# TensorE's semaphore increments in front of its product groups, taken out of a four-block graph network kernel

## The chip, the cores and the metric

One core of one Trainium2 chip runs the whole program in one launch. The metric is the device time of that launch in microseconds (us).

## The reference

The graph has 6,250 nodes with 16 features and 206,250 edges (100,000 in both directions, and a loop on each node), sorted by destination. Four blocks follow one another, each as `x = layernorm(x + block(x))`:

```python
# L0: messages from a tensor product of node and edge features, summed by destination row
m = silu(einsum('ei,ej,ijh->eh', x[src], edge_attr_8, W_msg_tp) * n1) @ W_msg_lin * n2
agg = segment_sum(m, row, n_nodes)
# ... update by a second tensor product of x and agg, silu, linear, residual

# L1: six graph convolutions (16-64-128-64, linear layers 64-32-3-32-64, then 64-128-64-16), leaky, tanh
agg = segment_sum(h[src] * norm[:, None], dst) + h * (dinv * dinv)[:, None]

# L2: maxima
h = segment_max(x[src] * edge_weight1, dst);  h @ W.T + b

# L3: two rounds; a 16x16 matrix for every edge out of a 13-32-256 network, mean, GRU
w = relu(edge_attr_13 @ w1 + b1) @ w2 + b2
m = einsum('ei,eio->eo', hx[src], w.reshape(-1, 16, 16))
hx = gru_cell(segment_sum(m, dst) * inv_deg[:, None], hx)
```

## The kernel before

The program is written engine by engine, each engine with its own list of instructions, and the engines meet only at semaphores. The edges stand in tiles of 128, and a batch is HT = 8 tiles; there are NB = 202 batches. Everything over the edges goes batch by batch, with buffers in pairs (`h = k % 2`), and gathers and sums are made as products with matrices of zeros and ones.

**The messages stage** (320 to 3,253 us in the profile) runs `messages` (lines 1003 to 1035) in a loop on the chip of 50 rounds of SL = 4 batches, and two batches behind it. For batch k TensorE does, in this order: `expand` for batch k+1 (L977, the tensor product on gathered rows); `compare` (L985) with `early` true; then three times (i = 0, 1, 2) 16 products of 392 columns that add placed messages into two banks (L1030), and ahead of the third of them `compare` with `early` false. ScalarE counts equal codes out of each `compare` in `count_equals` (L1310, four tiles each time), and VectorE turns the counts into places (L1933), casts, multiplies (L1888, L1905) and sums. GpSimd scatters finished rows (L859). Each `compare` waits until ScalarE has read the banks that it writes; each of the three parts of L1030 waits for a step of VectorE (HOTS, PLACE1, PLACED).

**The graph convolutions** (3,335 to 5,000 us) stream an adjacency matrix through a ring of buffers: `sum_block` (L1100) multiplies blocks of 28 tiles, its first product waiting for the block's transfer; `combine` (L1111) follows every group of blocks.

**Pass 7** (5,150 to 6,890 us, maxima) and **passes 8 and 9** (7,034 to 9,050 and 9,155 to 11,200 us, the two rounds of L3) gather rows with `gather8` (L900), turn them with `turn8` (L909), and add segments with `segments` (L885), whose output columns come from registers. `maxima` and `messages8` call these. In `messages8` TensorE makes the 16x16 matrices (L1234 for the bias, L1238) in two groups of banks as VectorE (L2287) has used the matrices of the batch before; VectorE multiplies and reduces (L2287, L2295), ScalarE compares indices (L1493, L1499), GpSimd gathers node rows (L841).

**The semaphore of this case.** `pe_go` (L349) is incremented by TensorE itself, by `pe.sem_inc(pe_go, 1)`, behind the waits that stand ahead of a group of products. It stands on 12 lines: 882 (`segments`), 896 (`gather8`), 1011, 1015, 1019 and 1026 (`messages`), 1068 (once), 1091 (`sum_block`), 1109 (`combine`), 1192 and 1201 (`maxima`) and 1232 (`messages8`). No engine waits for `pe_go`. `turn8` has waits without it, and so have `sum_block`'s waits for a transfer. VectorE has a semaphore of the same kind, `dve_go`.

The rows below name engines: PE is TensorE's products, PEld its weight loads, PEldq the records of TensorE's sequencer (the part of an engine that takes the program's instructions in order and hands them on) such as a separate semaphore instruction, SPq SyncE's issues of transfers.

Of the kernel before, what the change touches and what calls it, by code (L numbers as in the profile page):

```python
# [107 lines left out]
def build(nc, a, out):  # L108
# [12 lines left out]
    with ctx:  # L121
# [3 lines left out]
        def sem(name):  # L125
# [41 lines left out]
               for x in (arena[:, 6 * HE:6 * HE + HE // 2], acc[:, 4 * P:4 * P + HE // 2])]  # L167
# [112 lines left out]
                for j in range(2)]  # L280
# [65 lines left out]
        left_open = sem("left_open")  # L346
        hot8_made, picked, selected, turned, copied = [{p: sem(f"{x}{p}") for p in range(7, NPASS)}
                                                       for x in ("hot8_made", "picked", "selected", "turned", "copied")]
        pe_go = sem("pe_go")  # L349
        dve_go = sem("dve_go")  # L350
        r_out = sem("r_out")
        numbered = sem("numbered")
# [517 lines left out]
        def _(pe):  # L870
# [5 lines left out]
            def segments(p, k, h):  # L876

                pe.load(out_at, base[0:1, ds(k * HT + HT, HT)])
                outs = [pe.snap(r, min_val=0, max_val=2 * CH - 32) for r in out_at]
                pe.wait_ge(scl[p].sem, scl[p].at(k - 1, APER[p]))  # L880
                pe.wait_ge(vec[p].sem, vec[p].at(k + 1, LOWS7 if p == 7 else LOWS8))
                pe.sem_inc(pe_go, 1)
                for u in range(HT):
                    for x in (masked[h], rests[h], lows[h]):
                        last = mm(sums[:, ds(outs[u], 32)], hot[h][:, u, :], upper(x)[:, u * 32:(u + 1) * 32],  # L885
                                  start=False, stop=False)
                last.then_inc(ten[p].sem, 1)

            def gather8(p, j):

                if p == 7:
                    pe.wait_ge(hot8_made[p], j + 1)
                else:
                    pe.wait_ge(hot8_in[j % 2], hot8_count(p, j))
                pe.wait_ge(selected[p], j)
                pe.sem_inc(pe_go, 1)
                rows, hots = picked_rows[:, 0:gathers(p, j) * P], hot_of(p, j)
                for b in range(LAST):
                    for i in range(3):
                        mm(rows, x8[:, b, i, :], hots[:, b, :], start=b == i == 0, stop=False)  # L900
                last = mm(rows, x8[0:STACKED, LAST, 0, :], hots[0:STACKED, LAST, :], start=False, stop=True)
                last.then_inc(picked[p], 1)
# [99 lines left out]
            def messages(it, b, last_batch):  # L1002
                k, h = it * SL + b, b % 2
                pe.wait_ge(vec[0].sem, vec[0].at(k, HOTT))
                pe.wait_ge(vec[0].sem, vec[0].at(k, PROD))
                if last_batch:
                    pe.wait_ge(ten[0].sem, ten[0].at(k - 1, TPER[0]))
                    pe.sem_inc(ten[0].sem, 2)
                else:
                    pe.wait_ge(nodes_in[1 - h], nth(it, b + 1, 16 * HT))  # L1010
                    pe.sem_inc(pe_go, 1)
                    expand(k + 1, 1 - h)
                    pe.wait_ge(codes_in[1 - h], nth(it, b + 1, 16 * HT // R))
                    pe.wait_ge(scl[0].sem, scl[0].at(k, LATE_EQ + HT - 1))
                    pe.sem_inc(pe_go, 1)
                    compare(k + 1, 1 - h, True)
                for i, step in enumerate((HOTS, PLACE1, PLACED)):
                    pe.wait_ge(vec[0].sem, vec[0].at(k, step))
                    pe.sem_inc(pe_go, 1)
                    if i == 2:  # L1020
                        if last_batch:
                            pe.wait_ge(ten[0].sem, ten[0].at(k, LATE - 1))
                            pe.sem_inc(ten[0].sem, 1)
                        else:
                            pe.wait_ge(scl[0].sem, scl[0].at(k, EARLY_EQ + R - 1))
                            pe.sem_inc(pe_go, 1)
                            compare(k + 1, 1 - h, False)
                    for u in range(HT):
                        for half in range(2):
                            last = mm(halves[half], placed[h][:, i, u, :, :].rearrange("p a f -> p (a f)"),  # L1030
                                      hot_b[h * HT + u][:, half * (NB8 // 2):(half + 1) * (NB8 // 2)],
                                      start=False, stop=False)
                last.then_inc(ten[0].sem, 1)
# [31 lines left out]

            pe.wait_ge(agg_in, 1)
            pe.wait_ge(lin_open, 1)
            pe.sem_inc(pe_go, 1)
            spread_group(0)
            spread_group(1)  # L1070
            pe.wait_ge(positions, 4)
# [13 lines left out]
            def sum_block(p, G, j):  # L1085

                rows, W, par = piece(p), 3 * FEATURES[p], G % 2
                g, n = group_number(p, G), block_number(p, G, j)
                if p > 1 and G == 0:
                    chunks_done(pe, PHASES[p], min((j * SC + SC - 1) // 4, NC - 1), WAVES[PHASES[p]])  # L1090
                    pe.sem_inc(pe_go, 1)
                if j == 0:
                    if g >= 2:
                        pe.wait_ge(sum_vec, group_step(g - 2, REDUCED))
                    for bank in range(2):
                        mm(ps[:, 2 * par + bank, 0:2 * W], zero16[:, 0:P], zero16[:, 0:2 * W], start=True, stop=False)
                pe.wait_ge(blocks[n % RING], 16 * (n // RING + 1))
                for s in range(SC):
                    for u in range(GB):
                        last = mm(ps[:, 2 * par + u // 2, u % 2 * W:(u % 2 + 1) * W], ring[n % RING][:, s, u * P:(u + 1) * P],  # L1100
                                  rows[:, j * SC + s, :, :].rearrange("p k f -> p (k f)"),
                                  start=False, stop=(j == NCH - 1 and s == SC - 1 and u % 2 == 1))
                last.then_inc(blocks_used, 1)

            def combine(p, G):

                F, par = FEATURES[p], G % 2
                pe.wait_ge(sum_vec, group_step(group_number(p, G), REDUCED))
                pe.sem_inc(pe_go, 1)
                for u in range(GB):  # L1110
                    last = mm(ps[0:F, 6, u * P:(u + 1) * P], part[par][:, u * F:(u + 1) * F], pick[par][:, u, :],  # L1111
                              start=True, stop=True)
                last.then_inc(combined, 1)
# [67 lines left out]
            def maxima(k):  # L1181
# [7 lines left out]
                    turn8(p, k + AHEAD)  # L1189
                pe.wait_ge(loaded[h], load_count(p, k))  # L1190
                pe.wait_ge(scl[p].sem, scl[p].at(k - 1, RELU7))
                pe.sem_inc(pe_go, 1)
                for i in range(STRIPS):
                    last = mm(ps[32 * i:32 * i + 32, 7, 0:SE], w["f1"][32 * i:32 * i + 13, :], edges[h][32 * i:32 * i + 13, :],
                              start=True, stop=True)
# [2 lines left out]
                    gather8(p, k + AHEAD + 1)  # L1198
                segments(p, k - 1, 1 - h)
                pe.wait_ge(vec[p].sem, vec[p].at(k, SCAN))  # L1200
                pe.sem_inc(pe_go, 1)
                nc.tensor.transpose(ps[:, 6, 0:P], wk[:, HE:HE + P], w["ident"][:, :]).then_inc(ten[p].sem, 1)

            for k in range(NB):
# [14 lines left out]
            for p in (8, 9):  # L1219
# [6 lines left out]
                def messages8(k):  # L1226
# [2 lines left out]
                    pe.wait_ge(loaded[h], load_count(p, k))  # L1229
                    for strips, used in ((range(2), MUL[1]), (range(2, STRIPS), MUL[3])):  # L1230
                        pe.wait_ge(vec[p].sem, vec[p].at(k - 1, used))
                        pe.sem_inc(pe_go, 1)
                        for i in strips:
                            mm(ps[:, 4 + i, :], ones16[32 * i:32 * i + 32, :],  # L1234
                               bias3[32 * i:32 * i + 32, :].unsqueeze(1).to_broadcast([32, 2, 256]), start=True, stop=False)
# [1152 lines left out]
```

## Time and profile before

| | |
|---|---|
| time before, median of 3 runs | 11252.9 us |
| the three runs | 11252.9, 11231.1, 11258.11 us |
| the profiled execution | 11253.09 us |
| its span | 11251.3 us |
| granted TensorE clock over the span | 0.855 of full speed |
| TensorE products / weight loads busy | 79% / 51% of the span |
| VectorE / GpSimd / ScalarE busy | 55% / 40% / 32% |

The span is the stretch from the first to the last instruction; 1.8 us of the profiled execution's own time lie around it. Busy time is the time in which an engine executes; the time of a separate semaphore instruction isn't in it. No engine is busy throughout, so what sets the time is read from waits: what an engine waited for, and which part of a hand-off from one engine to the next is work.

### The profile page before, as it was taken

How to read it: one execution, taken by the hardware profiler on the slowest of the kernel's cores; microseconds unless marked ns; L12 is line 12 of the kernel's file. 1: busy time of each engine (PE TensorE's matmuls, PEld its weight loads, DVE VectorE, ACT ScalarE, POOL GpSimd, SP SyncE). 2: the span in 40 equal slices, each digit the busy share in tenths (PEclk: the TensorE clock that was granted, in tenths of full speed). 3: DMA queues.
4: the chain of work that ended last, by engine and by line, in shares of the span. 5: the costliest groups of instructions: out<-in, count | busy, mean ns of one | idle time of the engine just before them, and what ended most of it. 6: DMA issues, size and time to landing. Idle time of an engine off the chain costs nothing. (4 is left out here: it accounts for less than half of the span.)

```text
span 11251.3 us, 211389 instructions
## 1 busy us (share of the span) xinstructions
PE 8897.2 (79%) x72779; PEld 5698.2 (51%) x72910; DVE 6144.4 (55%) x11833; ACT 3561.2 (32%) x10701; POOL 4484.3 (40%) x4575
## 2 busy tenths in 40 slices
PE   0588888888878999956888885888788858788887
PEld 0345544555556878843444443555444535455544
DVE  2577766777753232223555553665666636666666
ACT  4234322333320010002444443333333323333334
POOL 1455555556530000005444553444444334444442
PEclk9899988899986999957888887888888878888888
DMA  9422233222239878973555553333333423333333
GB/s 317 151 76 81 80 86 88 80 80 80 80 122 368 311 251 313 337 310 116 157 158 159 159 159 108 109 105 106 107 105 108 113 68 105 108 105 107 106 107 90
DMA packets 998418, 1625.38 MB, mean 144 GB/s; under 512 B 253394, under 2 KB 787598, under 8 KB 997174
## 3 DMA queue, kind: packets, MB, share of 16 engines
q1 hardware_dynamic: 808244, 1542.53, 41.8%
q0 software_dynamic: 146240, 27.89, 3.0%
q10 hardware_dynamic: 43202, 44.90, 1.2%
q8 instruction: 496, 8.13, 0.3%
q14 instruction: 236, 1.93, 0.1%
HBM read 1324.07 MB, written 289.76 MB: 143 GB/s over the span
## 5 line engine op out<-in xcount | busy, mean ns | idle before, releaser
L841 POOL DMA_INDIRECT arena<-tab,x_all x2902 | 2747.6, 947 | 5074.9 <-DMA tab<-stage 2026.1
L859 POOL DMA_INDIRECT adj<-acc x1616 | 1683.0, 1041 | 1288.5 <-DVE acc L1933 747.2
L900 PE MATMUL ps<-invdeg,acc 128*128 128x384 bf16 (+1 forms) x5377 | 1369.2, 413 | 224.1 <-issue 216.2
L900 PE MATMUL ps<-dinv,acc 128*128 128x384 bf16 (+1 forms) x5404 | 1267.9, 387 | 324.5 <-issue 259.0
L1310 ACT ACTIVATE wide<-ps,not_all 128x128 bf16<-128x128 f32 x1616 | 658.2, 419 | 1535.6 <-remote 993.0
L900 PEld LDWEIGHTS ps<-invdeg,acc 128*128 128x128 bf16 x5454 | 621.3, 120 | 939.7 <-issue 738.7
L900 PEld LDWEIGHTS ps<-dinv,acc 128*128 128x128 bf16 x5454 | 591.0, 114 | 962.1 <-issue 745.6
L1493 ACT ACTIVATE arena<-w_iota,rel 128x128 f32<-128x128 f32 x3232 | 987.9, 388 | 13.5
L2287 DVE TENSOR_TENSOR dinv<-ps,arena 128x512 f32<-128x512 f32 x808 | 519.1, 684 | 784.6 <-remote 778.8
L2287 DVE TENSOR_TENSOR arena<-ps,arena 128x512 f32<-128x512 f32 x808 | 519.2, 684 | 725.8 <-remote 708.6
L1499 ACT ACTIVATE acc<-arena,unit 128x1024 bf16<-128x1024 f32 x303 | 347.9, 1148 | 1744.4 <-PE ps L1238 894.6
L1499 ACT ACTIVATE arena<-arena,unit 128x1024 bf16<-128x1024 f32 x303 | 347.9, 1148 | 1659.0 <-PE ps L1238 689.7
L977 PE MATMUL ps<-arena 128*128 128x128 f32 x3232 | 481.8, 289 | 381.1 <-issue 198.1
L909 PEld LDWEIGHTS ps<-x_all,dinv 128*128 128x128 f32 x3892 | 578.6, 222 | 397.6 <-issue 242.1
L909 PE MATMUL ps<-x_all,dinv 128*128 128x16 f32 x3892 | 640.3, 291 | 168.6 <-issue 121.9
L1888 DVE TENSOR_TENSOR arena<-ps,threes 128x1024 bf16<-128x1024 f32 x606 | 718.7, 1212 | 0.0
L1238 PE MATMUL ps<-w_w2b,arena 32*128 32x256 f32 x6464 | 668.4, 463 | 2.6 <-issue 2.4
L1100 PE MATMUL ps<-x_all,arena 128*128 128x192 bf16 (+1 forms) x8232 | 591.5, 233 | 91.9 <-DMA arena<-adj 91.7
L977 PEld LDWEIGHTS ps<-arena 128*128 128x128 f32 x3232 | 432.3, 200 | 446.3 <-issue 322.8
L1100 PE MATMUL ps<-arena 128*128 128x192 bf16 (+1 forms) x8232 | 602.1, 237 | 48.4 <-DMA arena<-adj 48.3
L1100 PEld LDWEIGHTS ps<-x_all,arena 128*128 128x128 bf16 x8232 | 553.3, 102 | 155.6 <-DMA arena<-adj 103.2
L1724 DVE SCALAR_TENSOR_TENSOR dinv<-x_all,ps 128x384 f32<-128x384 f16 (+1 forms) x606 | 384.0, 634 | 454.0 <-issue 218.3
(357 smaller groups left out, 14006.6 us busy)
## 6 DMA issues: line engine op xcount, KB each, us to landing
arena<-adj SPq DMA_DIRECT2D x588, 896.0 KB, 5.6
arena<-rels SPq DMA_DIRECT2D x202, 512.0 KB
arena<-tab SPq DMA_DIRECT2D x1616, 64.0 KB
invdeg<-hot_rows_of SPq DMA_DIRECT2D x150, 672.0 KB
dinv<-hot_rows_of SPq DMA_DIRECT2D x100, 896.0 KB
adj<-zero SPq DMA_DIRECT2D x28, 3136.0 KB
dinv<-hot_rows_of SPq DMA_DIRECT2D x102, 672.0 KB
x_all<-src_parts SPq DMA_DIRECT2D x202, 256.0 KB
```

The source lines that it names most:

```text
L841: pool.indirect_dma_start(G[b][:, u, :], None, TABLE[PHASES[p]], bass.IndirectOffsetOnAxis(ap=idx[:, t:t + 1], axis=0)).then_inc(gathered[ ...
L859: pool.indirect_dma_start(adj_cells, bass.IndirectOffsetOnAxis(ap=pair[:, t, 0:1], axis=0), pair16[:, t, 2:3], None).then_inc(celled[g], 16)
L900: mm(rows, x8[:, b, i, :], hots[:, b, :], start=b == i == 0, stop=False)
L909: last = mm(turned_rows[:, u * 16:(u + 1) * 16], picked_by[j % 2][:, u * P:(u + 1) * P], pick_f, start=True, stop=True)
L977: last = mm(ps[:, 2 + u // 4, (u % 4) * P:(u % 4 + 1) * P], hotT[h][:, u * P:(u + 1) * P], nodes0[h][:, u, :], start=True, stop=True)
L1100: last = mm(ps[:, 2 * par + u // 2, u % 2 * W:(u % 2 + 1) * W], ring[n % RING][:, s, u * P:(u + 1) * P], rows[:, j * SC + s, :, :].rearran ...
L1238: last = mm(ps[:, 4 + i, v * 256:(v + 1) * 256], strip[h][32 * i:32 * i + 32, v * P:(v + 1) * P], w["w2b"][32 * i:32 * i + 32, :], start=F ...
L1310: act_fn(junk[u % 2][:, 0:(u % R + 1) * P], equal_to(u), ACT.Relu, bias=not_all[:, :], accum_out=equals[h][:, u:u + 1]).then_inc(scl[0].se ...
L1493: last = act_fn(far2[:, u, :], w["iota"][:, :], ACT.Square, scale=-1.0, bias=r[:, tile(k, u):tile(k, u) + 1])
L1499: act_fn(hot[h][:, :, :], far2[:, :, :], ACT.Relu, scale=-2.0, bias=unit[:, :]).then_inc(scl[p].sem, 1)
L1888: tt(placed[h][:, i, :, :, :], hot_a[:, :, :].unsqueeze(3).to_broadcast([P, HT, A8, 16]), threes[h][:, :, i, :].unsqueeze(2).to_broadcast( ...
L2287: tt(products[h][:, q * 512:(q + 1) * 512].rearrange("p (u o i) -> p u o i", u=2, i=16), ps[:, 4 + q, :].rearrange("p (u o i) -> p u o i", ...
```

## The change

All twelve `pe.sem_inc(pe_go, 1)` and the semaphore itself are taken out. No product, no wait, no transfer and no line of another engine is changed, and the order of TensorE's products and weight loads is the same.

```diff
@@ segments
                 pe.wait_ge(scl[p].sem, scl[p].at(k - 1, APER[p]))
                 pe.wait_ge(vec[p].sem, vec[p].at(k + 1, LOWS7 if p == 7 else LOWS8))
-                pe.sem_inc(pe_go, 1)
                 for u in range(HT):
@@ gather8
                 pe.wait_ge(selected[p], j)
-                pe.sem_inc(pe_go, 1)
@@ messages
                     pe.wait_ge(nodes_in[1 - h], nth(it, b + 1, 16 * HT))
-                    pe.sem_inc(pe_go, 1)
                     expand(k + 1, 1 - h)
                     pe.wait_ge(codes_in[1 - h], nth(it, b + 1, 16 * HT // R))
                     pe.wait_ge(scl[0].sem, scl[0].at(k, LATE_EQ + HT - 1))
-                    pe.sem_inc(pe_go, 1)
                     compare(k + 1, 1 - h, True)
                 for i, step in enumerate((HOTS, PLACE1, PLACED)):
                     pe.wait_ge(vec[0].sem, vec[0].at(k, step))
-                    pe.sem_inc(pe_go, 1)
...
                             pe.wait_ge(scl[0].sem, scl[0].at(k, EARLY_EQ + R - 1))
-                            pe.sem_inc(pe_go, 1)
                             compare(k + 1, 1 - h, False)
@@ sum_block
                     chunks_done(pe, PHASES[p], min((j * SC + SC - 1) // 4, NC - 1), WAVES[PHASES[p]])
-                    pe.sem_inc(pe_go, 1)
@@ combine
                 pe.wait_ge(sum_vec, group_step(group_number(p, G), REDUCED))
-                pe.sem_inc(pe_go, 1)
@@ maxima
                 pe.wait_ge(scl[p].sem, scl[p].at(k - 1, RELU7))
-                pe.sem_inc(pe_go, 1)
...
                 pe.wait_ge(vec[p].sem, vec[p].at(k, SCAN))
-                pe.sem_inc(pe_go, 1)
                 nc.tensor.transpose(ps[:, 6, 0:P], wk[:, HE:HE + P], w["ident"][:, :]).then_inc(ten[p].sem, 1)
@@ messages8
                         pe.wait_ge(vec[p].sem, vec[p].at(k - 1, used))
-                        pe.sem_inc(pe_go, 1)
                         for i in strips:
```

What the lines become is seen in the two built programs. An instruction there holds one wait. Before, the waits ahead of an increment go, with the increment, into a separate semaphore instruction. Without the increment the wait stands on the next instruction, which is the first weight load of the group; where a group waits for two semaphores, one separate semaphore instruction stays, with one of the two waits, and the other wait stands on the weight load (in `segments`, on the first of the register instructions that work out the output columns). So the separate instruction is gone at L1015, L1019 and L1026 in all batches, at L1011 in about three of four, at L1109, at L1201, at five of the 35 of L1091, and in the second of the two groups of a batch of L1232. It stays, without its increment, at `segments`, at `gather8`, at L1192 and in the first group of L1232.

## Rows read from the trace of the kernel before

**Rows 1.** The page, busy time, share of the span and number of instructions.

```profile
PE 8897.2 (79%) x72779; PEld 5698.2 (51%) x72910; DVE 6144.4 (55%) x11833; ACT 3561.2 (32%) x10701; POOL 4484.3 (40%) x4575
```

**Rows 2.** Windows by stage: length, engines' busy us (instructions), clock, DMA share, GB/s.

```profile
320.00:3253.00 2933.00, 2427.53 (x14437) 1450.68 (x14438) 2031.42 (x3649) 941.47 (x3936) 1667.18 (x1600) 0.90 0.30 84
3335.00:5000.00 1665.00, 1460.06 (x17808) 1255.79 (x17809) 449.94 (x1053) 122.67 (x247) 0.00 (x0) 0.87 0.89 324
5150.00:6890.00 1740.00, 1514.34 (x11942) 822.76 (x12016) 961.31 (x3201) 802.13 (x2222) 818.19 (x860) 0.85 0.53 159
7034.00:9050.00 2016.00, 1640.29 (x13873) 1018.57 (x13898) 1255.23 (x1816) 749.35 (x2018) 854.50 (x906) 0.84 0.38 106
9155.00:11200.00 2045.00, 1642.34 (x13870) 1027.14 (x13895) 1251.04 (x1811) 747.80 (x2018) 872.56 (x926) 0.83 0.37 105
```

**Rows 3.** By source line, `messages`: semaphore instructions, ns min/median/max, first and last start.

```profile
L1011 PEldq EVENT_SEMAPHORE  x201: 51/51/51, 325.9 to 3249.3; - x101
...
L1015 PEldq EVENT_SEMAPHORE  x201: 51/51/2512, 329.9 to 3252.0; - x101
...
L1019 PEldq EVENT_SEMAPHORE  x606: 51/51/51, 330.4 to 3269.3; - x152
...
L1026 PEldq EVENT_SEMAPHORE  x201: 51/51/51, 333.2 to 3257.3; - x101
```

**Rows 4.** By source line, convolutions and passes 7 to 9: the same columns.

```profile
L882 PEldq EVENT_SEMAPHORE  x609: 51/2397/4675, 5156.6 to 11204.1; - x153
...
L896 PEldq EVENT_SEMAPHORE  x606: 51/51/45266, 5057.5 to 11171.1; - x152
...
L1109 PEldq EVENT_SEMAPHORE  x84: 51/51/51, 3352.9 to 4998.5; - x84
...
L1201 PEldq EVENT_SEMAPHORE  x202: 51/51/51, 5161.5 to 6883.3; - x101
...
L1232 PEldq EVENT_SEMAPHORE  x808: 51/51/51, 7030.3 to 11196.3; - x162
```

**Rows 5.** Waits: engine, tile, line, what it waited for, us, times, longest.

```profile
ACT wide L1310 <- remote: 993.0, 147, 16.4
...
DVE dinv L2287 <- remote: 778.8, 186, 4.5
...
DVE arena L2287 <- remote: 708.6, 183, 4.3
...
PE ps L985 <- ACT wide L1310: 155.3, 170, 1.6
```

**Rows 6.** Timeline around 1273 us: start, duration, engine, line, and idle before.

```profile
1272.87 0.21 ACT L1310 ACTIVATION_READ_ACCUMULATOR wide<-ps,not_all 128x1 f32 x1
1273.19 0.14 PEld L985 LDWEIGHTS ps<-arena 22*128 22x128 bf16 x4 [1.09 <-issue]
```

**Rows 7.** Timeline around 8027 us, `turn8`, where no `pe_go` stands.

```profile
8026.32 0.60 DVE L1724 SCALAR_TENSOR_TENSOR dinv<-x_all,ps 128x384 f32<-128x384 f16 x1
...
8026.98 0.74 PEld L909 LDWEIGHTS ps<-x_all,dinv 128*128 128x128 f32 x6 [0.40 <-DVE dinv L1724]
```

**Rows 8.** Timelines of TensorE alone at 4200 and at 3600 us.

```profile
4199.82 4.78 PE L1100 MATMUL ps<-x_all,arena 128*128 128x192 bf16 x56
...
3599.76 10.48 PE L1100 MATMUL ps<-x_all,arena 128*128 128x192 bf16 x125
```

**Rows 9.** Timelines, 1247 to 1257 us and around 1272 us.

```profile
1247.30 8.22 SPq L750 DMA_DIRECT2D arena<-tab  x8
...
1250.44 0.34 PE L985 MATMUL ps<-arena 22*128 22x128 bf16 x4
...
1257.13 0.37 ACT L1310 ACTIVATE wide<-ps,not_all 128x128 bf16<-128x128 f32 x1 [6.62 <-remote]
...
1272.03 1.82 SPq L755 DMA_DIRECT2D arena<-bits  x4
```

**Rows 10.** Groups of weight loads: count, busy us, mean ns, idle before them.

```profile
L1030 PEld LDWEIGHTS ps<-acc,arena 128*128 128x128 bf16 x2424 | 265.3, 110 | 242.4 <-issue 115.4
```

More of the change, by code:

```diff
@@ L348, in build @@
                                                        for x in ("hot8_made", "picked", "selected", "turned", "copied")]
-        pe_go = sem("pe_go")
         dve_go = sem("dve_go")
@@ L1231, in messages8 @@
                         pe.wait_ge(vec[p].sem, vec[p].at(k - 1, used))
-                        pe.sem_inc(pe_go, 1)
                         for i in strips:
```

## The prediction

> **What bounds the kernel now.** The page's first part comes first: TensorE's products are busy for 79% of the span, its weight loads for 51%, VectorE for 55% [rows 1]. No engine fills the span, so the windows by stage come next [rows 2]. Each stage has TensorE busy for 81 to 88% of its length (2427.53 of 2933 us in the messages stage, 1642.34 of 2045 us in pass 9), in every case more than any other engine. But TensorE isn't simply the bound. The waits show that the other engines stand still for what TensorE makes, and TensorE for them: ScalarE's counting (L1310) waits 993.0 us in 147 long waits, VectorE's products with the edge matrices (L2287) 778.8 and 708.6 us, all of them "remote", which is a release that the trace has no record of [rows 5]. One of these in full: TensorE's comparison (L985) starts at 1250.44 and ends at 1250.78, and ScalarE's L1310, which needs nothing but that comparison and its own work before, starts at 1257.13, after 6.62 us of waiting [rows 9]. So some hand-offs arrive long after the product that makes them, and the chain product, hand-off, ScalarE or VectorE, hand-off back is what sets a batch. In the convolutions the transfers (DMA share 0.89, 324 GB/s [rows 2]) stand beside TensorE.
>
> Within that, the lines of this change are read from the separate semaphore instructions. One that lasts 51 ns found its wait met when it came to it; a longer one held TensorE's sequencer until its release. In the messages stage all 201 of L1011, all 606 of L1019 and all 201 of L1026 last 51 ns, L1015 up to 2512 ns [rows 3]. In the passes L882 is late as a rule (median 2397 ns, up to 4675), L896 seldom (median 51), L1201 and L1232 never [rows 4].
>
> **The change, part by part.** Counted in the built programs, about 1,853 separate instructions go: about 150 at L1011, 201 at L1015, 606 at L1019, 201 at L1026, 404 of the 808 at L1232, 202 at L1201, 84 at L1109, 5 at L1091. The others of these lines stay and only lose their increment.
>
> *The hand-off where the wait is late and the instruction goes (L1015).* ScalarE's last L1310 ends at 1272.87 + 0.21 = 1273.08, and the weight load that it releases starts at 1273.19: 0.11 us through a separate instruction [rows 6]. The nearest row with the wait on the weight load itself is `turn8`: VectorE ends at 8026.32 + 0.60 = 8026.92, and the load starts at 8026.98: 0.06 us [rows 7]. That is 0.05 us, or the length of the instruction itself (51 ns). TensorE waits for this release 170 times [rows 5], and there are 201 such instructions: between 170 x 0.05 = 9 us and 201 x 0.06 = 12 us. This hand-off lies on the chain of the batch: ScalarE's late counting ends, the early comparison runs, and ScalarE's next counting waits for it (L1310). I take 11 us.
>
> *The instructions whose wait is met long before (L1011, L1019, L1026, L1201, L1232, L1109).* They sit in the sequencer, ahead of the products that still run. A met wait costs the sequencer 51 ns, and the sequencer has at least 16 products of some 0.17 us each between two of them (four L1030 products take 0.84 us of record and the whole stage gives TensorE 14,437 products in 2933 us, 0.20 us each [rows 2]). The work that hides them is TensorE's own queue of products. If that cover isn't there, each costs its 51 ns: 1,853 x 0.051 = 95 us is the most that this can give back, and zero the least. The nearest row is that all of them stand at 51 ns in stretches where the products run on, so I take zero.
>
> *The instructions that stay (L882, L896, L1192, the first group of L1232).* L882 is the one late wait of passes 7 to 9, and it keeps its separate instruction, since it waits for two semaphores. What goes is an increment that nobody waits for. In the same instruction it adds no time that the rows show: nothing.
>
> *Waits on weight loads, new.* Could a weight load that carries a wait be worse than a plain one? The convolutions have such loads already: each block of 28 products begins with one, without `pe_go`. A run of 56 products, two blocks, takes 4.78 us, 85 ns each, and a run of 125, more than four blocks, takes 10.48 us, 84 ns each [rows 8]. If each met wait cost a load's 0.1 us, the second run would be some 0.4 us longer than 125 times the product's time within a block. I see nothing of that size, and take zero. Its bound is a whole exposed load, and stands under rival C.
>
> The sum: 11253.09 (the profiled execution, which is the median of 11252.9 within 0.2 us) - 11 = 11242 us. That is -0.1%, below the 0.3% that a measurement of this kernel can tell from no change (the three runs before already spread by 0.24%).
>
> **The rivals.**
>
> *A, the forecast: only L1015's hand-off shortens.* 11242 us; with the runs' own spread 11220 to 11260.
>
> *B, faster: late hand-offs shrink because TensorE's sequencer and the semaphores have less to do.* The 6.62 us of [rows 9] aren't explained by work. In that same stretch SyncE's issues of transfers come slowly too: eight in 8.22 us, where four take 1.82 us at 1272 [rows 9], 1.03 against 0.46 us each. Something that the engines share delays small instructions and hand-offs there, and many removed events may lighten it. A price in proportion: the messages stage has 14437 + 14438 + 3649 + 3936 + 1600 = 38,060 records of work [rows 2]; 1,158 instructions and 1,209 increments go, 6.2% of that number. 6.2% of the 993.0 us of late counting is 62 us. In passes 8 and 9 the records are 32,511 and 32,520, and 1,616 increments and 404 instructions go, 3.1%; of 778.8 + 708.6 = 1487.4 us that is 46 us. All of both with L1015's 11 gives -119, 11134 us. I center it with half of the passes' part, since VectorE's wait there has other work of the batch beside it: 11 + 62 + 23 = 96, 11157 us. For it: the lateness is the largest thing in the waits, and its cause is in no row. Against it: the share removed is small, and a shared delay needn't go in proportion.
>
> The Trainium skill has a rule that would give B its mechanism: the page "NOTIFIC — the notification-queue block", section 7.1, says that the internal path for the records of instructions always holds back its producers rather than lose a record, and that this can throttle an engine. By it each removed instruction is a record less. That the profiled execution's time equals the median doesn't settle it, since no run here shows whether the other runs carry the same records.
>
> *C, slower: a weight load that carries a wait isn't taken ahead of the products that run.* A plain load is hidden beside the product before it. If the one with the wait is held until the products before it are done, its length is exposed once for every group whose wait moved onto it: in the messages stage L1011, L1026 and three of L1019, 5 per batch. 5 x 202 x 0.110 us [rows 10] = 111 us, less L1015's 11: 11353 us. It decides at about 0.01 us per load: above that, L1015's gain is eaten. For it: before, the sequencer had passed the wait by the time the load was queued, so the load was free to go ahead; afterwards it may not be. Against it: the runs of [rows 8]. The stage is busy with products for 83% of its time, so an exposed load would mostly count. The page "TensorE: Matmul & The Clock Gate" of the Trainium skill, section "Step-by-step: what each phase is for", has TensorE's queue pull weight loads ahead of products in flight, on conditions of row groups and of the background buffer; it says nothing on loads that wait, so it leaves C open rather than supporting it.
>
> *D: the change does nothing that is seen*, because L1015's 0.05 us is lost in another wait of the batch: 11253 us. It is inside A's range.
>
> **How the numbers follow.** A 0.43, B 0.36, C 0.18, D 0.03. B's chance is that high because it needs only one part of a large unexplained quantity. The predicted time is A's, 11242 us. The range goes from 11134, B's far end, taken as 11130, to 11300, which holds A, D, nearly all of B, and the part of C in which half a load or less is exposed: 0.43 + 0.03 + 0.31 + 0.05 = 0.82. A's own range is 11220 to 11260. Faster by over 0.3% means below 11219: B, and a little of A, 0.37. Within 0.3%: A and D, with some of B's near end, 0.42. Slower by over 0.3%, above 11287: C with what is left, 0.21.
>
> **What would show it.** In the profile of the changed kernel, right for A: L985's load begins 0.06 us behind ScalarE's last L1310, where it was 0.11; the semaphore instructions of L1015, L1019 and L1026 are gone; the messages stage is shorter by about 10 us, and the other stages by less than 10 each. Right for B: the wait "ACT wide L1310 <- remote" well below 993 us, L2287's below 1487, and passes 8 and 9 shorter although their late wait, L882, stands as before. Right for C: a gap of 0.1 us or more ahead of the first L1030 product of a part, and the messages stage longer by 100 us. What would make the prediction wrong is that the late hand-offs react to TensorE's semaphore instructions at all, in either direction: their 2,480 us are more than two hundred times the term that I count.

## The result and the profile after

| | before | changed |
|---|---|---|
| time, median of 7 runs each | 11252.9 us | 11311.5 us |
| lowest and highest | 11231.1, 11284.0 | 11288.5, 11338.0 |
| ratio of changed to before | | 1.0048, 95% interval 1.0031 to 1.0064 |
| span of the profiled execution | 11251.3 us | 11302.2 us |

The changed kernel is slower by 0.5%, some 55 us. The forecast was 11242 us with a range of 11130 to 11300: the time lies outside, on the other side. All lines behind L882 have moved up: L985 is now L982, L1030 is L1023, L1310 is L1297, L2287 is L2274.

The page's first part shows no work added; TensorE's products are even busy for a little less [rows 1]:

```profile
PE 8868.1 (78%) x72779; PEld 5648.2 (50%) x72910; DVE 6138.1 (54%) x11833; ACT 3567.3 (32%) x10701; POOL 4480.1 (40%) x4575
```

Where the time went is told by stage, each from the first to the last start of one line in the profiled execution (L1030 for the messages, L1100, L1194, L2287):

| us | messages | convolutions | pass 7 | pass 8 | pass 9 |
|---|---|---|---|---|---|
| before | 2944.2 | 1662.3 | 1726.8 | 2010.3 | 2003.8 |
| changed | 3000.3 | 1668.0 | 1724.1 | 2000.9 | 2000.5 |

The messages stage lost 56 us, passes 8 and 9 gained 13 together. In the trace by source line, the fields behind the count are ns min/median/max of one and the first and last start; the first two rows are L1030 of before, the last two L1023 of the changed kernel:

```profile
L1030 PE MATMUL ps<-acc,arena x2424: 326/329/534, 341.7 to 3274.1; 128*128 128x392 bf16 x187
...
L1030 PE MATMUL ps<-arena x1212: 326/329/534, 330.5 to 3261.0; 128*128 128x392 bf16 x174
```

```profile
L1023 PE MATMUL ps<-acc,arena x2424: 326/329/535, 342.2 to 3330.7; 128*128 128x392 bf16 x187
...
L1023 PE MATMUL ps<-arena x1212: 326/329/534, 331.0 to 3319.2; 128*128 128x392 bf16 x174
```

The products themselves are as long as before; only the last starts 57 us later. The median batch isn't longer either: 14.15 us from one batch's first L1030 to the next before, 14.12 now, and 16 products of a part take 2.50 us from the first start to the last in both. What changed is the mean, 14.61 to 14.89: batches longer than 17 us were 12 of 201 and are 25. Seen by part, the 606 parts of 16 products exceed their 2.5 us by 235 us in sum before and by 343 us now, and the time between the parts is 52 us less: more of the lost time falls into the parts. The waits of the changed kernel (columns as in [rows 5]) put it down to late counting, as there:

```profile
ACT wide L1297 <- remote: 1095.0, 153, 16.7
...
DVE dinv L2274 <- remote: 780.0, 186, 4.6
DVE arena L2274 <- remote: 701.7, 182, 4.3
...
PEld ps L982 <- ACT wide L1297: 159.1, 139, 2.0
...
PE ps L982 <- ACT wide L1297: 123.4, 127, 1.6
```

ScalarE's wait on "remote" is 102 us longer than in [rows 5], VectorE's two are 5.7 us shorter in sum, and the products' own wait for ScalarE's last counting is 123.4 where it was 155.3. That last difference isn't the term of the forecast: 127 waits are put down to it instead of 170, and the mean of one rose from 0.91 to 0.97 us. The term is the hand-off itself, and it came as forecast. In the timeline of the changed kernel:

```profile
1288.46 0.21 ACT L1297 ACTIVATION_READ_ACCUMULATOR wide<-ps,not_all 128x1 f32 x1
1288.73 0.11 PEld L982 LDWEIGHTS ps<-arena 22*128 22x128 bf16 x4 [1.49 <-ACT wide L1297]
```

1288.46 + 0.21 = 1288.67, and the load starts 0.06 us later, where it was 0.11 [rows 6]. Over all groups that were released within 0.4 us, the median is 114 ns before (184 groups) and 51 ns now (160).

One of the new long batches looks like this (timeline of the changed kernel; start, duration, engine, line, idle before):

```profile
754.17 0.70 SPq L749 DMA_DIRECT2D arena<-tab  x1
...
754.92 0.33 PE L1023 MATMUL ps<-invdeg,arena 128*128 128x392 bf16 x1 [0.24 <-issue]
...
755.66 0.10 PEld L1023 LDWEIGHTS ps<-invdeg,arena 128*128 128x128 bf16 x1 [0.95 <-issue]
...
756.38 0.33 PE L1023 MATMUL ps<-invdeg,arena 128*128 128x392 bf16 x1 [1.13 <-issue]
...
757.09 0.10 PEld L1023 LDWEIGHTS ps<-invdeg,arena 128*128 128x128 bf16 x1 [1.33 <-issue]
...
757.81 0.33 PE L1023 MATMUL ps<-invdeg,arena 128*128 128x392 bf16 x1 [1.10 <-issue]
...
770.13 0.37 ACT L1297 ACTIVATE wide<-ps,not_all 128x128 bf16<-128x128 f32 x1 [16.51 <-remote]
```

Load, product, load, product come 0.7 us apart (755.66, 756.38, 757.09, 757.81) with no wait between them, for 16 us, and ScalarE gets TensorE's comparison only when it ends. The profile calls it "issue": TensorE waits for nothing that it shows. I call these **slow stretches**. [rows 9] shows the same in SyncE. Counted in the trace, gaps of 0.6 us or more between the starts of two products in the messages stage are 519 before and 609 in the changed kernel; in the convolutions, where GpSimd does nothing, gaps of 0.6 to 0.8 us are 6 in both.

### The profile page after: what moved, and what is told of

Same layout as the page of the kernel before. It is cut to its first block and busy times, and to the rows that moved or that the text cites. A ratio compares the mean times of both kernels' runs of the same rounds, so it can differ in the third digit from the quotient of the medians.

```text
span 11302.2 us, 209539 instructions
## 1 busy us (share of the span) xinstructions
PE 8868.1 (78%) x72779; PEld 5648.2 (50%) x72910; DVE 6138.1 (54%) x11833; ACT 3567.3 (32%) x10701; POOL 4480.1 (40%) x4575
## 5 line engine op out<-in xcount | busy, mean ns | idle before, releaser
L897 PE MATMUL ps<-invdeg,acc 128*128 128x384 bf16 (+1 forms) x5377 | 1333.2, 402 | 264.8 <-issue 165.3
L1297 ACT ACTIVATE wide<-ps,not_all 128x128 bf16<-128x128 f32 x1616 | 656.5, 418 | 1593.5 <-remote 1095.0
L2274 DVE TENSOR_TENSOR dinv<-ps,arena 128x512 f32<-128x512 f32 x808 | 518.4, 683 | 784.9 <-remote 780.0
L2274 DVE TENSOR_TENSOR arena<-ps,arena 128x512 f32<-128x512 f32 x808 | 518.5, 683 | 717.0 <-remote 701.7
L1091 PE MATMUL ps<-x_all,arena 128*128 128x192 bf16 (+1 forms) x8232 | 594.1, 234 | 93.6 <-DMA arena<-adj 93.5
L1225 PE MATMUL ps<-w_w2b,arena 32*128 32x256 f32 x6464 | 639.5, 449 | 0.7 <-issue 0.7
L1091 PE MATMUL ps<-arena 128*128 128x192 bf16 (+1 forms) x8232 | 603.1, 237 | 46.5 <-DMA arena<-adj 46.3
L1091 PEld LDWEIGHTS ps<-x_all,arena 128*128 128x128 bf16 x8232 | 556.0, 103 | 156.7 <-DMA arena<-adj 103.0
```

What stands on the lines that cost most here:

```text
L1225: last = mm(ps[:, 4 + i, v * 256:(v + 1) * 256], strip[h][32 * i:32 * i + 32, v * P:(v + 1) * P], w["w2b"][32 * i:32 * i + 32, :], start=F ...
L1297: act_fn(junk[u % 2][:, 0:(u % R + 1) * P], equal_to(u), ACT.Relu, bias=not_all[:, :], accum_out=equals[h][:, u:u + 1]).then_inc(scl[0].se ...
L2274: tt(products[h][:, q * 512:(q + 1) * 512].rearrange("p (u o i) -> p u o i", u=2, i=16), ps[:, 4 + q, :].rearrange("p (u o i) -> p u o i", ...
```

## The experiments

The runs came in sets, each on one chip with the kernel before beside them, and only within a set are times compared; in three sets there were hardly any slow stretches and the kernel before took 8,242 to 8,245 us, in the others it took 11,246 and 11,096 us.

### Which part: e1 to e4, a set without slow stretches

e1 takes out the increments of `messages` alone, e2 those of all other lines, e4 L1019 alone. e3 is the changed kernel with, at the four lines of `messages`:

```diff
-                    pe.sem_inc(pe_go, 1)
+                    pe.nop(nofuse=True)
```

which builds to the same separate semaphore instructions with their waits, without the increment.

> Only the four increments of `messages` (L1011, L1015, L1019, L1026) are taken out; the other eight stay. Theory W (a wait that moves onto a weight load in the messages stage, instead of standing in a separate instruction, brings more of the slow stretches): the whole of the change's +56 us in the messages stage, 11,305 to 11,320 us. Theory E (the change's loss is everywhere and the stages only differ by chance): half of it or less, 11,270 to 11,290 us. Theory I (the missing increments do it, not the place of the wait): as W.

> The eight increments outside `messages` are taken out, the four in it stay. Theory W: 11,240 to 11,255 us, the messages stage as before and passes 8 and 9 together up to 13 us shorter, as in the changed kernel. Theory E: 11,270 us or more.

> The changed kernel, but in `messages` each increment is replaced by an empty instruction that holds the wait: in the built program a separate semaphore instruction with the wait and without an increment, at the same 1,209 places. Theory W: the messages stage as in the kernel before, 11,240 to 11,255 us. Theory I (increments): the messages stage as in the changed kernel, 11,300 to 11,320 us.

> Only L1019 (the three waits of VectorE's steps ahead of the parts of L1030) loses its increment: 606 of the 1,158 separate instructions of the messages stage go. Theory W, each place alike: about half, +25 to +35 us, 11,280 to 11,290 us. Theory L (only the late wait L1015 matters, where TensorE's sequencer now runs on past the wait): no change, 11,245 to 11,260 us. Theory P (the loop's length and place in the code decide): any size, unrelated to the number of instructions.

Before 8245.3 us. Measured: e1 8244.6 (ratio 1.0000, 0.9991 to 1.0009), e2 8246.6 (0.9995, 0.9985 to 1.0004), e3 8243.5 (0.9998, 0.9988 to 1.0007), e4 8240.6 (0.9994, 0.9985 to 1.0003). None moves the time, so the set tells nothing of the 55 us, but much of what the 11,253 us are. The messages stage took 2,200 us instead of 2,944, pass 7 1,180 instead of 1,727, passes 8 and 9 about 1,265 each instead of 2,007; only the convolutions kept theirs (1,664 to 1,670 beside 1,662). In the messages stage of e1 gaps of 0.6 us or more are 8. And L1015, which I had read as late, is never late here. In e2 it is L1013:

```profile
L1013 PEldq EVENT_SEMAPHORE  x201: 51/51/51, 330.4 to 2512.0; - x101
```

### The change itself, and added records: f1 to f3, g1 to g4, sets without slow stretches

f1 and g4 are the changed kernel. f2 and f3 are the kernel before and the changed one, both with

```diff
+                        for _ in range(60):
+                            sp.sem_inc(extra, 1)
...
+                            if (i, u, half) != (2, HT - 1, 1):
+                                last.then_inc(extra, 1)
```

the first behind SyncE's loads of a batch, the second at L1030. g2 has `pe.nop(nofuse=True)` at all twelve lines, g1 eight further increments behind each L1019, g3 40 increments by ScalarE and those of the products.

> The changed kernel itself, beside the kernel before. In the runs of e1 to e4 the kernel before took 8,245 us, the late hand-offs of up to 16 us were all but absent, and no part of the change moved the time. Theory S (the +56 us of the changed kernel lies only in those slow stretches, where TensorE and SyncE take 0.7 us for each instruction): where they are absent, the changed kernel is within 0.2% of the kernel before, 8,235 to 8,255 us; where they are there, it is 0.3 to 0.6% slower in the messages stage alone. Theory T (all twelve together cost what no part alone costs): +40 to +60 us even without them.

> The changed kernel once more, beside the others of this set, since the kernel before has taken 11,253 us in one set of runs and 8,245 us in others. Where the set takes 8,245 us, no difference (within 0.2%). Where it takes 11,253 us, +40 to +70 us by every theory that takes the first measurement as it is; a theory that puts the +56 us down to chance expects less than 20 us.

f1: 8246.2 us, ratio 1.0002 (0.9993 to 1.0011); g4: 8250.8, 1.0007 (0.9997 to 1.0016). The messages stage is 2197.5 and 2197.1 us. Without slow stretches the change costs nothing that can be told, as theory S had it. The window of f1 over its messages stage (columns as in [rows 2]) shows why no hand-off counts there: TensorE is busy for 97% of it.

```profile
333.00:2530.00 2197.00, 2127.30 (x14497) 1351.47 (x14496) 1994.58 (x3653) 938.27 (x3941) 1627.45 (x1601) 0.98 0.42 112
```

> The kernel before, with semaphore increments that nobody waits for added in the messages stage: 60 by SyncE for each batch, behind its issues of transfers, and one by each of 47 of the 48 products of L1030. Theory R (the slow stretches come when the recording of instructions and semaphore changes has more than it can take; the trace of the kernel before kept 99,274 semaphore changes, that of e1 183,584): slow stretches of 0.7 us per TensorE instruction appear in the messages stage, which grows from 2,200 us by hundreds of us. Theory Q (the slow stretches have another cause): the messages stage stays within 30 us of 2,200 us.

> The changed kernel with the same added increments. Theory R, with the change's +56 us as something that slow stretches bring: longer than f2 by 20 to 100 us in the messages stage. Theory R, with fewer instructions to record as a gain: shorter than f2 by 20 to 100 us. Theory Q: equal to f2 within 15 us.

f2: 8764.1 us, f3: 8754.9 (4 runs each, ranges overlap). The messages stage grew to 2,710 and 2,708 us, but with 13 and 11 gaps of 0.6 to 0.8 us, where the trace of the kernel before in the first set has 191. What it waits for is another thing: SyncE's 60 instructions stand ahead of its next loads, and VectorE waits for those (L1905 of f2 is L1900 of the kernel before, the comparison that needs `rels`).

```profile
DVE arena L1905 <- DMA arena<-rels: 518.3, 141, 31.9
```

So f2 isn't the test that it was to be. What it shows is by accident: with late counting on the path without slow stretches, hand-offs at L985 of 113 ns (181 groups) in f2 and of 50 ns (178) in f3, the moved waits cost nothing either; f3 is shorter by 9 us, which is within the runs' spread. Nor does the hand-off's own saving show there: 180 times 63 ns would be 11 us, and the stages of the two traces differ by 2.

> All twelve increments replaced by an empty instruction that holds the wait: in the built program the same separate semaphore instructions as before, without their increments (as many as in the kernel before). With slow stretches in the runs: theory W (a wait on a weight load) expects the time of the kernel before, theory I (the increments) that of the changed kernel. Without them: no difference by either.

> The kernel before with eight more increments behind each L1019: 24 separate semaphore instructions more per batch, 4,824 in all, where the change takes away 1,158. If a separate instruction whose wait is met is hidden by the products queued ahead of it, as the prediction has it: no change, within 15 us. If each costs its 51 ns: +246 us. With slow stretches in the runs, and theory B (time in proportion to the instructions that TensorE's sequencer handles): +200 us or more.

> The kernel before with 40 increments more per batch by ScalarE between its late and its early counting, and one by nearly every product of L977 and L1030: some 95 semaphore changes and 40 instructions more per batch to record, and nothing at SyncE. Theory R (slow stretches come when recording can't keep up): slow stretches of 0.7 us per TensorE instruction, and the messages stage longer by more than 100 us. Theory Q (they have another cause): no such stretches; at most what ScalarE's 2 us per batch cost by themselves, 0 to 100 us.

g2: 8254.8 us, 1.0014 (1.0005 to 1.0024); g1: 8257.6, 1.0015 (1.0005 to 1.0024); g3: 8245.1, 0.9997 (0.9988 to 1.0007). g1's messages stage is 2,208 us, 11 us more than g4's, for 5,982 separate instructions more (4,824 added and the 1,158 that g4 lacks): 2 ns each instead of 51. So the cover that the prediction named, TensorE's queue of products, holds here. g3 brings no slow stretches on. g2's 10 us aren't in the messages stage (2,197.7), and I can't say what they are.

### With slow stretches: h1 to h4

Here the kernel before took 11,246.3 us. h3 takes out L1015's increment alone, h4 all but that one.

> Only L1015's increment, that of the early comparison, is taken out. Without slow stretches L1015 is never late, and the time is that of the kernel before within 10 us. With them: the hand-off's gain of 0.06 us each gives -10 us if the prediction's term is all there is; if the late wait on the weight load is what brings the loss, +40 us or more.

> The changed kernel with L1015's increment kept, and the other eleven taken out. Without slow stretches: the time of the kernel before within 10 us. With them: +0 to +15 us if L1015 carries the loss, +40 us or more if the moved waits of the other lines do.

| | time, us | ratio, 95% | messages, us | gaps of 0.6 us or more there |
|---|---|---|---|---|
| h3 | 11270.1 | 1.0034 (1.0012 to 1.0055) | 2966.1 | 589 |
| h4 | 11310.3 | 1.0072 (1.0044 to 1.0100) | 3036.3 | 681 |

The traces of the first set, before and changed, have 519 and 609 gaps for 2944 and 3000 us. In these four traces the stage is the longer, the more such gaps there are. h3's trace is of the fastest of its six runs (11252.8 us). The loss repeats in another set. It isn't L1015 alone, for h4 keeps L1015 and has at least as much of it, and L1015 isn't free of it either: in h3 the hand-off is 51 ns (144 groups), worth 9 us, and the kernel is slower all the same.

h1 and h2 are the kernel before and the changed one with the additions of g3 and, by TensorE behind each tile of L1030:

```diff
+                        for _ in range(2):
+                            pe.sem_inc(extra, 1)
```

> The kernel before with, per batch of the messages stage, 48 separate increments more by TensorE (two behind each tile of L1030), one by nearly every product of L977 and L1030, and 40 by ScalarE: some 142 semaphore changes and 88 instructions more to record in each 10.5 us. Theory R (recording that can't keep up makes the slow stretches): semaphore records are lost in number, stretches with 0.7 us per TensorE instruction appear, the stage is longer by more than 300 us. Theory Q: no such stretches, and at most 100 us for the added instructions themselves.

> The changed kernel with the same additions. If slow stretches appear in h1: theory W, longer than h1 by 20 to 100 us; if time follows the number of records, shorter than h1 by 10 to 60 us. If none appear: within 15 us of h1.

h1: 11531.7 us (11527.0 to 11540.6), +285 us, the messages stage 3250.4. h2: 11503.4 us (11484.0 to 11526.5), stage 3230.0; the gaps of 0.6 us or more are 584 and 572, about as many as in h3 and fewer than in h4, so their number doesn't follow the time here. Where slow stretches are, added instructions and semaphore changes do cost; without slow stretches half of TensorE's separate instructions cost 11 us (g1), and all the rest of the additions nothing (g3). And with 48 separate instructions per batch left between the products in either kernel, the change's sign turns: h2 is 28 us shorter than h1. So the moved waits bring no loss in slow stretches when that many separate instructions stand between the products.

### What of the three parts does it: k1 to k3, with slow stretches

k1 is g2, k3 is e1. k2 is the changed kernel with as many separate instructions as before, but behind the groups and without a wait:

```diff
                     expand(k + 1, 1 - h)
+                    pe.sem_inc(extra, 1)
...
                     compare(k + 1, 1 - h, True)
+                    pe.sem_inc(extra, 1)
...
                                       start=False, stop=False)
+                    pe.sem_inc(extra, 1)
```

> As g2: all twelve increments are gone, all the separate instructions stay and hold the waits. With slow stretches in the set (the kernel before near 11,250 us): if the loss comes from the moved waits or the missing instructions, the messages stage is as before, total within 25 us of it; if it comes from the missing increments, +40 to +70 us. Without slow stretches (near 8,245 us): within 12 us, and it tells nothing of the loss.

> The changed kernel with one separate increment behind each group of products in `messages` (six per batch, on a semaphore that nobody waits for): as many separate instructions as before, but every wait on the weight load. With slow stretches: if the place of the wait brings the loss, +40 to +70 us as in the changed kernel; if the number of separate instructions between the groups is what counts, the kernel before within 25 us. Without slow stretches: within 12 us.

> As e1: the increments of `messages` alone are taken out. With slow stretches: +50 to +75 us, the whole loss of the changed kernel and a little more, since passes 8 and 9 were 12 us shorter in it. Without slow stretches: within 10 us.

The kernel before took 11096.1 us here, and it has no trace in this set.

| | time, us | ratio, 95% | messages | pass 7 | passes 8 + 9 |
|---|---|---|---|---|---|
| k1 | 11054.3 | 0.9962 (0.9934 to 0.9989) | 3035.6 | 1704.8 | 3771.9 |
| k2 | 11060.2 | 0.9960 (0.9937 to 0.9983) | 3024.9 | 1702.7 | 3773.5 |
| k3 | 11154.2 | 1.0049 (1.0026 to 1.0072) | 3068.3 | 1711.9 | 3819.5 |

The first rows below are L1030's products in k1, k2 and k3, with the last start at the end of the times, then ScalarE's late counting:

```profile
L1029 PE MATMUL ps<-acc,arena x2424: 326/329/534, 342.4 to 3365.3; 128*128 128x392 bf16 x187
...
L1027 PE MATMUL ps<-acc,arena x2424: 326/329/534, 340.1 to 3352.8; 128*128 128x392 bf16 x187
...
L1026 PE MATMUL ps<-acc,arena x2424: 326/329/534, 342.8 to 3399.3; 128*128 128x392 bf16 x187
...
ACT wide L1309 <- remote: 1165.9, 145, 16.4
...
ACT wide L1302 <- remote: 1095.2, 135, 16.4
...
ACT wide L1306 <- remote: 1151.5, 134, 16.3
```

k3 repeats the loss, +58 us, with the increments of `messages` alone gone. k1 and k2 both are shorter than the kernel before, by 42 and 36 us. Between k3 and them lie 100 and 94 us: 33 and 43 in the messages stage, where they keep the separate instructions, and 48 and 46 in passes 8 and 9 and 7 and 9 in pass 7, where they have no `pe_go` and k3 has it. That k1 and k2 are faster than the kernel before therefore comes from the later passes as far as these traces tell; what they say of `messages` rests on the 33 and 43 us. So:

- The missing increments alone aren't the loss: k1 has none, and its messages stage is 33 us shorter than k3's.
- The moved waits alone aren't the loss: k2 has them all on the weight loads (hand-off 51 ns in 160 groups), and its messages stage is 43 us shorter than k3's.
- What k1 and k2 share and k3 lacks are the separate instructions: keeping as many goes with 33 to 43 of some 58 us. The other 15 to 25 us stay open. The split by stage is from one trace of each kernel, while single runs of k3 lie up to 97 us apart (11097.7 to 11194.6 us). That k3 is slower than k1 and k2 is clear by the intervals of the table; how the 94 to 100 us fall to the stages isn't.
- How the loss comes about isn't shown. The 606 parts of 16 products exceed 2.5 us by 547 us in k3, by 457 and 421 in k1 and k2, the same way as in the first set (343 against 235). But gaps of 0.6 us or more are 701, 673 and 704 in k1, k2 and k3, and ScalarE's late counting is longest in k1. Some 20 to 30 us of k3's surplus are products at the lower clock (1,141 of 9,696 last over 500 ns, where k1 has 971 and k2 1,005; they start 0.33 instead of 0.17 us apart); in the first set the clock isn't it, for there the changed kernel has fewer of them, 1,059 against 1,109.
- Outside `messages` the change goes with a gain here: passes 8 and 9 are 47 us shorter. In the first set they were 13 us shorter, in h2 against h1 17, in h4 against h3 less than 1. The changed kernel itself, traced twice without slow stretches (f1, g4), took 2523.0 and 2553.9 us there, so that 13 or 17 us can't be told from chance.
- One rival has no run: where the instructions lie. k1 and k2 keep not only the number of separate instructions but nearly the length of TensorE's loop and the places of what is in it; the changed kernel, h4 and k3 shorten it by the same edit. The expectation of e4 names this as theory P, and e4 met no slow stretches. Separate instructions moved to the end of the loop's body, with slow stretches in the set, would tell the two apart.

## Why the prediction was wrong, point by point

**The bound.** "Some hand-offs arrive long after the product that makes them" was right, and it was the main thing: in sets without slow stretches 3,000 us are gone, and the waits on "remote" at L1310 with them. In f1 ScalarE's counting waits for TensorE by name:

```profile
ACT wide L1297 <- PE ps L982: 787.8, 292, 84.6
```

What failed is that I took the chain of [rows 5] as the kernel's: in the sets without slow stretches L1015 is never late. One reading was off too: TensorE is busy for 80% of pass 9 (1642.34 of 2045 us), not 81 or more.

**L1015's hand-off** came out as worked out: 114 to 51 ns, about 150 times, 9 to 10 us where 11 were forecast. But h3, which has this and nothing else, is 0.34% slower. A saving on a chain counts only if nothing else on it reacts, and the same edit took a separate instruction from TensorE's stream. In f3 against f2, with 180 late hand-offs and hardly a slow stretch, the saving wasn't seen either.

**"The instructions whose wait is met long before ... I take zero"** is the step that failed. Its bounds were 0 and a gain of 95 us. What the runs showed in its place is a loss: taking the increments of `messages` out costs 58 us (k3), and by k1 and k2 some 33 to 43 of them go with the separate instructions, outside both ends. The cover that I named is real where there are no slow stretches (g1: 2 ns for each instruction of 51), though not as I described it: between L1015 and the first L1019 stand four products and not 16, and between the third L1019 and L1026 none. In sets with slow stretches the kernel with fewer of these instructions was slower, by a mechanism that stays open, and I had left out a loss with no row that excluded it: there is none that shows what TensorE's sequencer does in such a stretch with fewer of them.

**"The instructions that stay ... nothing"** was perhaps wrong in size too: in the last set passes 8 and 9 are 48 us shorter in k1, where only the increments are gone there, and 46 in k2, where the separate instruction of L1232's second group is gone as well. These are single traces, and the 13 us of the first set can't be told from chance.

**"Waits on weight loads, new"** came to the right value by a comparison that couldn't have told: the run of 56 products and that of 125 both have one such wait for 28 products, so an exposed load would lengthen both alike. The trace settles it: at 4200 and at 3600 us the products start 82 or 83 ns apart within a block and from one block to the next.

**Rival B** (late hand-offs shrink) named what reacts, the late hand-offs, and had the sign right in passes 8 and 9 of the last set, where 46 us were its far end; in the first set VectorE's two waits fell by 5.7 us only. In the messages stage, where it had 62 us of gain, they grew: ScalarE's wait rose from 993.0 to 1095.0 us. Time doesn't go in proportion to the instructions that TensorE hands on. The rule of the Trainium skill that was cited with it ("NOTIFIC — the notification-queue block", section 7.1: the path for records may throttle an engine) is neither shown nor excluded. For it speaks that the recorder is short where the stretches are slow: the trace of the kernel before kept 99,274 semaphore changes, that of f1, with 3,756 fewer increments, 180,461; and ahead of the stretch at 754 us they fall from some 55 in 1.5 us (740 to 744 us) to fewer than 20 (from 747 us), before TensorE slows. That order in time is weak, for few records are the rule: in the messages stage of the kernel before 1,548 of 1,963 stretches of 1.5 us have fewer than 20, and in 1,075 of these TensorE starts six or more products. h1's +285 us speak for it too. Against it: f2 and g3 added records and brought no stretch on, and fewer records made the messages stage longer.

**Rival C** (an exposed weight load) had the right sign and less than twice the size, by a mechanism that isn't there. It wanted a gap of 0.1 us ahead of each part; from the start of the first part's last product to that of the second part's first it is 0.166 us in the median, before and after. f1, h2 against h1, and k2 against the kernel before each move the waits of `messages` and lose nothing in time.

**What is open:** why the kernel with fewer separate instructions in TensorE's stream is slower where there are slow stretches, whether their number or the place of the code counts, what makes these stretches in one set and not in another, and the last 15 to 25 us of the messages stage. That needs runs with the kernel before traced several times in a set with slow stretches.

## What to carry to other kernels

Ask first whether the largest wait of a profile belongs to the kernel: engines that took 0.7 us for instruction after instruction with no wait between them, and a releaser that is only "remote", didn't here; a saving read off a chain inside such stretches isn't a forecast. Where a shared and unexplained delay is on the path, removing small instructions beside it can go either way, so both signs belong in the range, however well the instructions are hidden. And time a small edit in several sets: this one is 0.5% slower in one and within 0.1% in two others.

## What the runs showed of the hardware

- A wait on a weight load hands over in 50 ns after ScalarE's end, one in a separate semaphore instruction ahead of it in 113 ns (f3 and f2, 163 of 178 and 166 of 181 groups within 20 ns of that).
- A separate semaphore instruction whose wait is met cost TensorE's stream 2 ns when products were queued (g1), though it is recorded with 51.
- The same program took 8,245 us in one set of runs and 11,253 in another, with the granted clock over the span at 0.953 and 0.855 of full speed. In the slower one single instructions of TensorE take 0.7 us each, for up to 16 us at a time (754 to 770 us above), and SyncE's issues 0.7 us (754.17) to 1.0 us [rows 9], in the stages in which GpSimd moves data, and not in the convolutions, though TensorE handles the most instructions per us there [rows 2].
- In slow stretches the kernel with fewer separate semaphore instructions in TensorE's stream was the slower one four times (h3: 0.3%; changed kernel, h4, k3: 0.5 to 0.7%). With 48 such instructions per batch added to both it was the faster one, by 28 us (h2 against h1).
